# A vision tower's first stage on one core: patch tokens and the first normalization in one stage, with TensorE reading the pixels from the image tile

## The reference

```python
patches = X.reshape(B, C, N_PATCHES, PATCH, N_PATCHES, PATCH)
patches = patches.transpose(0, 2, 4, 1, 3, 5).reshape(B, N_PATCHES * N_PATCHES, IN_D)
tokens = jnp.einsum('bpi,hi->bph', patches, W) + b
cls = jnp.broadcast_to(class_token[None, :, :], (B, 1, HID))
tokens = jnp.concatenate([cls, tokens], axis=1)
return tokens * pos_embed[None, :, :]
...
m = jnp.mean(x, axis=axis, keepdims=True)
v = jnp.var(x, axis=axis, keepdims=True)
return (x - m) / jnp.sqrt(v + eps)
```

## Time and profile before

| | before |
|---|---|
| time, median of 3 runs | 4192.47 us (4190.81 to 4195.63) |
| the profiled execution's own time | 4191.02 us |
| its span in the trace | 4189.3 us |
| token stage, to its last store | 250.6 us |
| first normalization, from there to its last product | 42.0 us |
| next stage's first transfer issued | 294.18 us |
| mean granted TensorE clock | 0.944 of full |

### The profile page before, as it was taken

One profiled execution on the slowest core, in us unless ns is written; L12 is line 12 of the kernel. 1 busy time (PEld: TensorE's weight loads), 2 busy tenths in 40 slices (PEclk: granted clock), 3 DMA queues, 4 the chain that ended last, 5 costly groups with the idle time before them and its releaser, 6 DMA issues. The chain is left out here.

```text
span 4189.3 us, 98294 instructions
## 1 busy us (share of the span) xinstructions
PE 3695.9 (88%) x36068; PEld 2265.2 (54%) x36068; DVE 2841.8 (68%) x5015; ACT 2150.3 (51%) x4378; POOL 1278.5 (31%) x1076
## 2 busy tenths in 40 slices
PE   5869689979988998952999999999999959999998
PEld 4645346646655655631555555555555527666665
DVE  8966568858858857876666666666666664555555
ACT  4536437737746755755444444444444445555554
POOL 0027537627726736744000000000000003444443
PEclk8889899989999999975999999999999978999999
DMA  8910100010010011025111111111111131111111
GB/s 174 176 33 0 52 18 2 1 56 2 0 42 16 0 42 32 0 87 157 46 50 48 45 48 50 48 44 48 49 49 43 49 103 52 54 53 53 53 53 30
DMA packets 392895, 205.07 MB, mean 49 GB/s; under 512 B 151221, under 2 KB 386474, under 8 KB 392106
## 3 DMA queue, kind: packets, MB, share of 16 engines
q1 hardware_dynamic: 392354, 203.09, 18.9%
q10 hardware_dynamic: 392, 0.03, 0.0%
HBM read 145.55 MB, written 57.51 MB: 48 GB/s over the span
## 5 line engine op out<-in xcount | busy, mean ns | idle before, releaser
L1827 PE MATMUL banks<-l_w,l_xs 128*64 128x512 f16 x6240 | 722.3, 381 | 15.0 <-DVE l_xs L1875 14.2
L1827 PE MATMUL banks<-l_w,l_hs 128*64 128x512 f16 x6144 | 705.8, 379 | 1.7 <-DVE l_hs L1881 1.7
L1827 PEld LDWEIGHTS banks<-l_w,l_xs 128*64 128x64 f16 x6240 | 344.6, 110 | 330.7 <-issue 25.6
L1827 PEld LDWEIGHTS banks<-l_w,l_hs 128*64 128x64 f16 x6144 | 348.3, 110 | 316.7 <-DVE l_hs L1881 2.2
L194 POOL MEMSET h_ident<- 128x128 f32 x1 | 0.2, 204 | 1444.3 <-POOLq L81 1444.3
L985 POOL TENSOR_TENSOR ax_p<-ax_p,ax_ri 128x520 f32<-128x520 f32 (+1 forms) x256 | 320.0, 1251 | 267.4 <-DVE ax_ri L1185 267.4
L1932 DVE SCALAR_TENSOR_TENSOR l_gates<-banks,l_unscale,l_bias 128x1024 f32<-128x1024 f32 x260 | 333.8, 1284 | 96.1 <-PE banks L1827 94.7
L1988 ACT ACTIVATE l_gates<-l_gates 128x768 f32<-128x768 f32 x260 | 219.1, 843 | 347.4 <-DVE l_gates L1932 347.4
L2259 PE MATMUL banks<-h_mem,h_w 128*128 128x320 f16 x2496 | 357.9, 300 | 1.0 <-DMA h_mem<-mem_scratch 1.0
L2554 ACT ACTIVATE h_work<-banks,h_bias,h_factor 128x320 f32<-128x320 f32 x312 | 192.3, 616 | 262.8 <-PE banks L2259 259.1
L2259 PEld LDWEIGHTS banks<-h_mem,h_w 128*128 128x128 f16 x2496 | 244.4, 98 | 94.9 <-issue 1.6
(11 more groups left out here) (306 smaller groups left out, 7180.4 us busy)
## 6 DMA issues: line engine op xcount, KB each, us to landing
image<-in_x_dram SPq DMA_DIRECT2D x192, 196.0 KB
l_x<-x_scratch SPq DMA_DIRECT2D x130, 256.0 KB, 3.0
mem_scratch<-l_hs SPq DMA_DIRECT2D x520, 64.0 KB, 1.9
h_mem<-mem_scratch SPq DMA_DIRECT2D x104, 320.0 KB, 3.7
x_scratch<-x_out SPq DMA_DIRECT2D x4, 4160.0 KB, 16.4
raw_in<-in_L_ffn_attn_in_w_dram SPq DMA_DIRECT2D x4, 768.0 KB, 4.5
h_scratch<-x_out SPq DMA_DIRECT2D x1, 2080.0 KB, 6.5
z_scratch<-z SPq DMA_DIRECT2D x1, 2080.0 KB, 11.6
```

The source lines that it names most:

```text
L1827: mm = pe.matmul(ps[d * HALF:(d + 1) * HALF, 2 * z + n, :], lhsT, w_of[e][:, d, kk, b, n * 512:(n + 1) * 512], start=(kk == 0 and turn_ == ...
```

## The change

`tokens_stage` and the first `norm_stage` become one block. `image` now has 128 partitions and four slots (the fourth lies in the `ring` tile, which is idle then), `packed` is gone, and TensorE's products read a pixel column straight from the image tile (`column`, a step of 28 elements). Columns 21 to 27 are still moved to partitions 96 to 127, now inside the image tile: one part by ScalarE, two by VectorE (L393, L394). Partitions 64 to 127 of each slot are zeroed first, and channel 2 of the first four chunks waits for that. A slot is loaded again when the chunk's products are done (`summed`). The normalization runs in spans of one chunk (260 columns), interleaved with the chunks. The loops are written out.

```diff
-def tokens_stage(nc, signals, ps, io, h0, ident, w_rows):
+def tokens_stage(nc, signals, shared, ps, io, h0, z, ident):
 
     XI = 4
-    SLOTS = 2
-    TRIPS = IMAGES // XI // SLOTS
+    SLOTS = 4
+    CHUNKS = IMAGES // XI
     NP = GRID * GRID
+    SPAN = XI * SEQ
     WHOLE = 21
     SPLIT = ((0, 32), (32, 64), (64, ROWS))
...
-        image = sb("image", [ROWS, SLOTS, XI, GRID, SIDE])
-        packed = sb("packed", [P, SLOTS, WHOLE, XI * NP])
+        w_rows = z[:, 0:ROWS * PATCH]
+        own = sb("image", [P, SLOTS - 1, XI, GRID, SIDE])
+        image = [own[:, s] for s in range(SLOTS - 1)]
+        image.append(shared.ring[:, 0:XI * GRID * SIDE].rearrange("p (b g w) -> p b g w", b=XI, g=GRID))
...
+        center = sb("n1_center", [P, P])
+        mean = sb("n1_mean", [P, P])
+        eps = sb("n1_eps", [P, 1])
+        xc = sb("n1_xc", [P, 2, SPAN])
+        sq = sb("n1_sq", [P, 2, SPAN])
+        sd = sb("n1_sd", [P, 2, SPAN])
+        rs = sb("n1_rs", [P, 2, SPAN])
...
 
-        def whole(s):
-
-            return (packed[0:ROWS, s].rearrange("p q (r j) -> p q r j", j=GRID),
-                    image[:, s].rearrange("p b g (j q) -> p q (b g) j", q=PATCH)[:, 0:WHOLE])
+        def column(s, q):
+
+            return image[s].rearrange("p b g (j q) -> p q (b g) j", q=PATCH)[:, q]
 
         def part(s, k):
 
             lo, hi = SPLIT[k]
-            return (packed[HIGH:HIGH + hi - lo, s, k:WHOLE:len(SPLIT)].rearrange("p q (r j) -> p q r j", j=GRID),
-                    image[lo:hi, s].rearrange("p b g (j q) -> p q (b g) j", q=PATCH)[:, WHOLE:PATCH])
+            view = image[s].rearrange("p b g (j q) -> p q (b g) j", q=PATCH)
+            return view[HIGH:HIGH + hi - lo, k:WHOLE:len(SPLIT)], view[lo:hi, WHOLE:PATCH]
+
+        span = lambda a, n: a[:, n * SPAN:(n + 1) * SPAN]
...
-            def load(chunk, s):
-                for c in range(CHANNELS):
+            def load(n, channels):
+                s = n % SLOTS
+                for c in channels:
                     for b in range(XI):
-                        src = io["x"][ds(chunk * XI + b, 1), c].rearrange("a (g p) w -> p (a g) w", p=PATCH)
-                        sp.dma_start(image[c * PATCH:(c + 1) * PATCH, s, b], src).then_inc(loaded[s], 16)
-
-            for s in range(SLOTS):
-                load(s, s)
-            with sp.Fori(0, TRIPS - 1) as i:
-                for s in range(SLOTS):
-
-                    sp.wait_ge(packed_act, BASE + i * SLOTS + s + 1)
-                    sp.wait_ge(packed_dve, BASE + i * SLOTS + s + 1)
-                    load((i + 1) * SLOTS + s, s)
+                        src = io["x"][n * XI + b, c].rearrange("(g p) w -> p g w", p=PATCH)
+                        sp.dma_start(image[s][c * PATCH:(c + 1) * PATCH, b], src).then_inc(loaded[s], 16)
+
+            for n in range(0, SLOTS, 2):
+                load(n, range(CHANNELS - 1))
+                load(n + 1, range(CHANNELS - 1))
+                sp.wait_ge(padded, BASE + n // 2 + 1)
+                load(n, (CHANNELS - 1,))
+                sp.wait_ge(padded_pool, BASE + n // 2 + 1)
+                load(n + 1, (CHANNELS - 1,))
+            for n in range(SLOTS, CHUNKS):
+                sp.wait_ge(summed, BASE + n - SLOTS + 1)
+                load(n, range(CHANNELS))
 
         @block.gpsimd
         def _(pool):
             make_identity(pool, ident, id_zero, id_done)
             pool.wait_ge(id_done, BASE + 1)
-            pool.memset(packed[64:P, 1], 0.0).then_inc(padded, 1)
+            pool.memset(image[1][64:P], 0.0).then_inc(padded_pool, 1)
+            pool.wait_ge(padded_pool, BASE + 1)
+            pool.memset(mean[:, :], 1.0 / P).then_inc(ready, 1)
+            pool.memset(eps[:, :], EPS).then_inc(ready, 1)
+            pool.memset(center[:, :], -1.0 / P).then_inc(zero, 1)
+            pool.wait_ge(zero, BASE + 1)
+            pool.affine_select(out=center[:, :], in_=center[:, :], compare_op=ALU.not_equal, fill=1.0 - 1.0 / P,
+                               base=0, pattern=[[-1, P]], channel_multiplier=1).then_inc(ready, 1)
+            pool.wait_ge(ready, BASE + 3)
+            pool.memset(image[3][64:P], 0.0).then_inc(padded_pool, 1)
+            pool.wait_ge(padded_pool, BASE + 2)
+            for n in range(CHUNKS):
+                pool.wait_ge(inverted, BASE + n + 1)
+                pool.tensor_tensor(span(z, n), xc[:, n % 2, :], rs[:, n % 2, :], ALU.mult).then_inc(normed, 1)
 
...
             pe.wait_ge(kept, BASE + turns + 1)
-            with pe.Fori(0, TRIPS) as i:
-                for s in range(SLOTS):
-                    pe.wait_ge(packed_act, BASE + i * SLOTS + s + 1)
-                    pe.wait_ge(packed_dve, BASE + i * SLOTS + s + 1)
-
-                    pe.wait_ge(stored, BASE + i * SLOTS + s - 1)
+            pe.wait_ge(ready, BASE + 3)
+            for n in range(CHUNKS + 2):
+                if n < CHUNKS:
+                    pe.wait_ge(moved_act, BASE + n + 1)
+                    pe.wait_ge(moved_dve, BASE + n + 1)
+                    if n >= 2:
+                        pe.wait_ge(stored, BASE + n - 1)
                     for q in range(WHOLE):
-                        m = pe.matmul(ps[:, s, 0:XI * NP], w_cols[:, q, :], packed[:, s, q, :],
+                        m = pe.matmul(ps[:, n % 2, 0:XI * NP], w_cols[:, q, :], column(n % SLOTS, q),
                                       start=(q == 0), stop=(q == WHOLE - 1))
                     m.then_inc(summed, 1)
+                if 1 <= n <= CHUNKS:
+                    pe.wait_ge(stored, BASE + n)
+                    if n >= 3:
+                        pe.wait_ge(copied, BASE + n - 2)
+                    pe.matmul(ps[:, 2 + (n - 1) % 2, 0:SPAN], center[:, :], span(h0, n - 1), start=True,
+                              stop=True).then_inc(centered, 1)
+                if n >= 2:
+                    pe.wait_ge(squared, BASE + n - 1)
+                    if n >= 4:
+                        pe.wait_ge(rooted, BASE + n - 3)
+                    pe.matmul(ps[:, 4 + n % 2, 0:SPAN], mean[:, :], sq[:, n % 2, :], start=True, stop=True).then_inc(varied, 1)
 
         @block.scalar
         def _(act):
-            act.wait_ge(padded, BASE + 3)
-            with act.Fori(0, TRIPS) as i:
-                for s in range(SLOTS):
-                    act.wait_ge(loaded[s], BASE + (i + 1) * 16 * CHANNELS * XI)
-
-                    act.wait_ge(summed, BASE + i * SLOTS + s - 1)
-                    for k in range(2):
-                        to, of = part(s, k)
-                        op = act.copy(to, of)
-                    op.then_inc(packed_act, 1)
+            act.wait_ge(ready, BASE + 3)
+            for n in range(CHUNKS + 3):
+                if n < CHUNKS:
+                    s = n % SLOTS
+                    act.wait_ge(loaded[s], BASE + (n // SLOTS + 1) * 16 * CHANNELS * XI)
+                    act.copy(*part(s, 0)).then_inc(moved_act, 1)
+                if 2 <= n < CHUNKS + 2:
+                    m = n - 2
+                    act.wait_ge(centered, BASE + m + 1)
+                    if m >= 2:
+                        act.wait_ge(normed, BASE + m - 1)
+                    act.copy(xc[:, m % 2, :], ps[:, 2 + m % 2, 0:SPAN]).then_inc(copied, 1)
+                    act.wait_ge(copied, BASE + m + 1)
+                    if m >= 2:
+                        act.wait_ge(varied, BASE + m - 1)
+                    act.activation(sq[:, m % 2, :], xc[:, m % 2, :], ACT.Square).then_inc(squared, 1)
+                if n >= 3:
+                    m = n - 3
+                    act.wait_ge(varied, BASE + m + 1)
+                    if m >= 2:
+                        act.wait_ge(inverted, BASE + m - 1)
+                    act.activation(sd[:, m % 2, :], ps[:, 4 + m % 2, 0:SPAN], ACT.Sqrt, bias=eps[:, 0:1]).then_inc(rooted, 1)
 
         @block.vector
         def _(dve):
-            dve.memset(packed[64:P, 0], 0.0).then_inc(padded, 1)
-            dve.memset(w_cols[64:P], 0.0).then_inc(padded, 1)
-            dve.wait_ge(padded, BASE + 3)
+            dve.memset(image[0][64:P], 0.0).then_inc(padded, 1)
+            dve.memset(w_cols[64:P], 0.0).then_inc(w_padded, 1)
+            dve.wait_ge(w_padded, BASE + 1)
             for g in range(turns):
                 dve.wait_ge(turned, BASE + g + 1)
                 now = ps[0:ROWS, g % 4, :].rearrange("p (j m) -> p j m", j=4)
@@ -322,6 +376,8 @@
                     op = dve.tensor_copy(w_cols[HIGH:HIGH + hi - lo, at:at + len(SPLIT) * (3 - here) + 1:len(SPLIT), :],
                                          now[lo:hi, here:4, :])
                 op.then_inc(kept, 1)
+                if g == 0:
+                    dve.memset(image[2][64:P], 0.0).then_inc(padded, 1)
             dve.wait_ge(turned, BASE + turns + 1)
             dve.tensor_copy(pos[:, :], ps[:, 0, 0:SEQ]).then_inc(kept, 1)
             dve.wait_ge(kept, BASE + turns + 1)
...
-
-            def pack(i, s):
```

(41 more changed lines are left out.)

20 lines of the change are left out of this document (8 added, 12 removed).

## The result

The changed kernel took 4285.06 us, the median of 4 runs (4281.13 to 4287.09), against 4191.67 us for the kernel before (4 runs, 4190.81 to 4195.63): a ratio of 1.022, with a 95% interval from 1.0202 to 1.0237. It is slower by 93 us. The forecast was 4146 us; the time lies outside its range and beside the rival "TensorE becomes the bound, at VectorE's 1.87 ns", which gave 4283. The profiled execution took 4287.09 us with a span of 4285.4, 96.1 us more than before.

What follows compares the result with a forecast made beforehand. Loads and VectorE's copies were taken as the bounds, then an uncovered normalization; load -6.9, copies -7.5, products +1.8, normalization -33.9 make -46.7 us from 4191.0, 4144.3, plus 1.5 to the median: 4146 us. Own range 4138 to 4158, full range 4136 to 4262.

Steps and rivals of the forecast that it cites:

- TensorE becomes the bound, at VectorE's 1.87 ns: Projection products: strided columns at 1.87 ns make a turn 21.2 us, the stage end 383, total 4283 us; chance 0.09.
- the one on the products: Last chunk's 42 records on TensorE: no penalty for strided columns, burst 11.0 us, +1.8 us with the hand-over.
- the transposes: Weight transposes in the kernel before: 84 strided columns in 0.11 us, at most 1.3 ns each, taken as evidence against a penalty.
- the slower cases: Projection products: strided columns at half rate, 4261 us, chance 0.13, or at VectorE's rate, 4283 us, chance 0.09.
- the last landing: Image loads: four slots bring chunks 13.3 us apart, the last at 221.5 instead of 228.4, -6.9 us; bounds 217.3 to 228.4.
- the copies: Moving columns 21 to 27 inside the image tile by VectorE and ScalarE: 12.1 us becomes 4.6, -7.5 us.
- the last products: Last chunk's burst of 42 records on TensorE: 11.0 us, since bursts begin below full clock after a pause.
- the tail: Normalization behind the last product: a store, four reciprocals in a row and GpSimd's last product, 8.6 us for 42.5, -33.9 us.
- The sum of the stage: End of the fused stage: 221.5 + 4.6 + 0.1 + 11.0 + 8.6 = 245.8 us against 292.55, -46.7 us.
- The start: Zeroing and first loads: VectorE's preparation ends near 26.8 us, chunk 0 lands near 30.9, both hidden by TensorE's slack.
- SyncE's wait: Before reloading an image slot: the wait for summed costs nothing while TensorE keeps pace, with 24 us of cover.
- a stall of instruction supply: Sign of error: TensorE stalling on instruction supply because the loops are written out beside a full DMA; no size given.

Runs made afterwards that it cites:

- experiment 6: Kernel before plus unused bursts of products on a zero-filled tile ahead of its first transposes; fp32 stream 467 ns a record stepped, 216 contiguous.
- experiment 4: Kernel before with VectorE's copy of 84 x 5376 issued as three copies of every third pixel column; 4181.88 us, ratio 0.9971.
- experiment 1: Changed kernel with TensorE reading 256 image elements side by side instead of a pixel column, so tokens sum other pixels; 4162.77 us, ratio 0.9929.
- Experiment 8: Changed kernel's fusion with packed kept, normalization one chunk behind, store ahead of the copies, products started third by third; 4140.91 us, ratio 0.987.

## Why the prediction was wrong

**The failed step** is the one on the products: "So TensorE's side is not held to the rate of the others, and I take no penalty." It was inferred from the transposes, and it failed twice over. The row was on the weight load and the change is on the stream, which pays its full price even in a transpose (233 ns a record). And in a transpose the fp32 weight load costs half of what it does in a product, at most 0.92 ns a column, as experiment 6 shows; 84 of them hide behind 128 streamed columns. The prediction named the first objection ("they read through the weight load, not the stream") and still gave the slower cases 0.22 together. What the runs showed in its place: 467 ns a record, 1.82 ns a column, and a burst of 19.75 us instead of 11.0. The rates of the other engines, 1.87 and 1.95 ns, were nearer to that than the row of TensorE's own, but for VectorE that was luck: experiment 4 has the same strided read at 1.12 ns.

**The rival's working** came out nearly right: a turn of 21.2 us was said, and 325.6 / 16 = 20.35 came (36.26 to 361.9); the end at 383, and it was 374.3. That its 4283 us met the 4285 within 2 is partly chance, since the stage ended 9 us earlier than it said and 13.9 us arose behind the stage, which nothing in the prediction foresaw.

**The other terms**, read where TensorE does not bound (experiment 1): the last landing at 225.4 instead of 221.5, because the loads came at 13.6 us a chunk and not at 13.3, still between the bounds; the copies 4.1 us instead of 4.6 (VectorE 2.06 and 2.03, ScalarE 3.53, so a strided write in the image tile costs nothing on either); the last products 9.3 instead of 11.0, since that burst ran at full clock (others of the same run took 10.99); the tail 12.4 from the last store instead of about 8.4. The sum of the stage would have been 251.3 instead of 245.8. Even without the step in the stream the forecast of 4146 would have been missed: experiment 1 took 4162.8 us, above the 4158 of its own range, for the 12.0 us behind the stage. (By its own terms that upper end is 4156: 228.4 + 8 + 0.1 + 11.0 + 8.6 = 256.1.)

**The tail** had the right queue and the wrong rhythm. Four reciprocals do stand behind the last store, but the first three start 3.9 us apart and not back to back; only the fourth follows at once: ScalarE's copy of a span waits for GpSimd's multiplication of the span two before (2.71 us idle in the row of 368.89 above), since the tiles are two deep. Reciprocal, multiplication, copy, square and root are a ring of 3.9 us. Experiment 8 has a backlog of two spans instead of four and a tail of 6.0 us.

**The start** was not hidden in the changed kernel: TensorE is the bound from its first burst at 36.26 us, so every delay ahead of that reaches the end. That rested on "TensorE has slack in every period", the same step that failed. VectorE's preparation ended at 29.2 us and not at 26.8. **SyncE's wait** for the products, costed at nothing "while TensorE keeps pace", became 156.3 us, since TensorE did not. Nor was a stall of instruction supply the error in this stage: TensorE ran without a gap. Of the changed kernel's 96 us of span, then, 82 are the stepped stream less the gains of the fusion (123 less 41, by experiment 1), and 13.9 arise behind the stage and go with where VectorE's instructions lie: 5.4 us of longer scalings at the port, the rest gaps and clock, not told apart.

## What to carry to other kernels

Removing a copy that packs data moves the stride to whoever reads next. Look up what that engine pays in the very role and mode (streamed or stationary, product or transpose) in which it will read. Where no row has it, neither a row of another role nor the rate of another engine stands for it; a burst of a dozen such products ahead of the real work, as in experiment 6, measures it. From a step of four fp32 elements on, TensorE's stream ran at half its rate here or below, and in 16 bits, at steps of 28 and 56 elements, at a quarter. Copies that are hidden under the loads are cheap: the same fusion with the packed tile kept gained 0.9% (0.3% of it from copying in thirds), and 1.3% with products that start on parts of it. When a change shortens the lag of a pipeline, write down the new loop's length before its tail. And a few microseconds that appear in a stage whose code did not change can come from where its instructions now lie: add some waits that are already met and measure again before looking for a cause in the change.

## What the runs showed of the hardware

- TensorE's stream in fp32 at most steps from 16 to 112 bytes: 1.69 to 1.88 ns an element; more at 80, 88, 96 and 108 bytes (2.07, 2.28, 2.49 and 1.98). In 16 bits 1.71 ns at 56 bytes and 1.82 at 112, as in fp32.
- A stepped fp32 weight load: 1.8 ns a column in a product, at most 0.92 in a transpose.
- VectorE copied 84 x 5376 in 10.05 us and the same elements as three copies of every third pixel column in 6.0.
- GpSimd's multiplication of 260 columns took 0.73 us alone and 2.02 us when a copy of VectorE had begun 0.12 us ahead of it (118.50 and 118.62 in the chunk above).
- Eight waits more in VectorE's program made a kernel 11 us faster.
